# Two network layers in one kernel: one block for both halves, a new opening order, and GpSimd powers in pairs

## The reference, cut to what matters

```python
# first layer
xn = layernorm(x)
s  = silu(xn @ w_gate.T)                    # 1376 wide
s  = keep the larger half of |s| in each row, others 0
s  = (s * (xn @ w_up.T)) @ w_down.T
g  = silu(xn @ ternary(weight).T + bias)
x  = x + s * g
# second layer
xn = layernorm(x)
h  = xn @ Win.T + bin                       # 64 wide
for l in range(4):
    y = silu(layernorm(h, l1w, l1b))
    y = sconv(y)        # y convolved over time with the powers of a complex number p per channel
    h = h + y * sc_lin
    y = layernorm(h, l2w, l2b)
    h = h + silu(y @ W1.T + b1) @ W2.T + b2
s  = layernorm(h) @ Wout.T + bout
g  = silu(xn @ (W + mix of 16 low-rank products).T + bias)
x  = x + s * g
```

## Time and profile before

| | us |
|---|---|
| median of 3 runs | 642.12 (641.61 to 645.01) |
| the profiled execution | 643.55 |
| its span in the profile | 641.7 |
| PE busy | 598.7 (93%) |
| DVE busy | 506.0 (79%) |
| ACT busy | 339.1 (53%) |
| POOL busy | 194.9 (30%) |

### The profile page before, as it was taken

One profiled execution on the slowest core, in us unless ns is written; L12 is line 12 of the kernel. 1 busy time (PEld: TensorE's weight loads), 2 busy tenths in 40 slices (PEclk: granted clock), 3 DMA queues, 4 the chain that ended last, 5 costly groups with the idle time before them and its releaser, 6 DMA issues. The chain is left out here.

```text
span 641.7 us, 8820 instructions
## 1 busy us (share of the span) xinstructions
PE 598.7 (93%) x2852; PEld 464.1 (72%) x2852; DVE 506.0 (79%) x932; ACT 339.1 (53%) x571; POOL 194.9 (30%) x303
## 2 busy tenths in 40 slices
PE   8969999999999999999999999999698899999775
PEld 6857887887888888888888888877566555555432
DVE  7998799897888788789788778677575787877655
ACT  6758477267438428627734752848362444445320
POOL 2422002001001000200200100489884666664334
PEclk9979999999999999999999999999796999999887
DMA  8802000210020030020010001460300000000015
GB/s 359 304 13 67 1 1 1 66 34 2 23 75 0 0 98 0 0 98 0 0 64 34 0 1 67 148 221 4 64 4 0 1 0 1 1 1 1 1 65 196
DMA packets 17194, 32.35 MB, mean 50 GB/s; under 512 B 3238, under 2 KB 3750, under 8 KB 17164
## 3 DMA queue, kind: packets, MB, share of 16 engines
q1 hardware_dynamic: 17164, 31.99, 14.3%
HBM read 24.63 MB, written 7.35 MB: 50 GB/s over the span
## 5 line engine op out<-in xcount | busy, mean ns | idle before, releaser
L857 DVE TENSOR_SCALAR_CACHE_REDUCE junk_d<-k_buf,cand 128x1376 int8<-128x1376 f32 x56 | 91.8, 1640 | 0.3
L650 ACT ACTIVATE junk_a<-k_buf,cand 128x1376 int8<-128x1376 f32 x56 | 80.5, 1437 | 0.6
L1197 PE MATMUL ps_a<-wd_hi,zt_hi 128*128 128x512 f32 (+1 forms) x176 | 71.9, 408 | 0.2 <-DVE zt_lo L976 0.2
L629 ACT ACTIVATE s_buf<-ps_a 128x1376 f32<-128x1376 f32 x16 | 21.1, 1318 | 93.9 <-PE ps_a L1164 89.4
L1197 PE MATMUL ps_a<-wd_hi,zt_lo 128*128 128x512 f32 (+1 forms) x176 | 69.2, 393 | 0.0
L1197 PE MATMUL ps_a<-wd_lo,zt_hi 128*128 128x512 f32 (+1 forms) x176 | 68.8, 391 | 0.0
L527 POOL TENSOR_TENSOR xres<-xres,gate 128x512 f32<-128x512 f32 x12 | 22.4, 1866 | 130.9 <-DVE gate L983 130.9
L519 POOL TENSOR_TENSOR rstd<-var_eps,expo 128x2 f32<-128x2 f32 x7 | 4.9, 706 | 164.9 <-DVE var_eps L779 164.9
L1164 PE MATMUL ps_b<-wu_hi,xt_hi 128*128 128x512 f32 (+1 forms) x192 | 52.4, 381 | 0.0
L1164 PE MATMUL ps_a<-wg_hi,xt_hi 128*128 128x512 f32 (+1 forms) x192 | 52.0, 379 | 0.0
L1164 PE MATMUL ps_a<-wg_lo,xt_hi 128*128 128x512 f32 (+1 forms) x192 | 50.7, 372 | 0.5 <-DVE wg_lo L762 0.4
(11 more groups left out here) (249 smaller groups left out, 1414.7 us busy)
## 6 DMA issues: line engine op xcount, KB each, us to landing
xres<-in_x SPq DMA_DIRECT2D x8, 512.0 KB, 3.3
out<-arena SPq DMA_DIRECT2D x16, 256.0 KB, 2.1
xin<-in_x SPq DMA_DIRECT2D x7, 512.0 KB, 4.0
x_scratch<-xres SPq DMA_DIRECT2D x6, 514.0 KB, 4.0
arena<-x_scratch SPq DMA_DIRECT2D x3, 1028.0 KB, 12.6
m_buf<-in_wg_t SPq DMA_DIRECT2D x2, 688.0 KB, 4.8
k_buf<-in_wg_t SPq DMA_DIRECT2D x2, 688.0 KB, 7.6
m_buf<-in_wu_t SPq DMA_DIRECT2D x2, 688.0 KB, 7.4
```

What stands on the lines that cost most here:

```text
L629: act.activation(s_buf[:, t, :], ps_a[:].rearrange("p a n -> p (a n)")[:, 0:INNER], ACT.Silu).then_inc(s_ready, 1)
L650: act.activation(junk_a[:], k_buf[:, 1, :], ACT.Sign, bias=c, scale=-1.0, accum_out=below[:, 1:2]).then_inc(act_step, 1)
L857: dve.tensor_scalar(junk_d[:], k_buf[:, 0, :], c, -float(DROP), ALU.is_lt, ALU.add, accum_out=e).then_inc(cnt_dve, 1)
L1197: last = pe.matmul(ps_a[:, t, :], zs, ws[0:rows, c, :], start=(c == 0 and n == 0), stop=(c == CHUNKS - 1 and n == 2))
```

## The change

- **One block.** The two blocks become one; each engine runs its first-layer program and then its second-layer program, with no barrier between. The SBUF order of buffers is changed so that `xt`, `row_f`, `row_r`, `ones_r`, `tbig` and the first tables lie over buffers that are free early; `w_down` and what is needed longest lie behind them. `tokens(i)` gets waits for the PSUM banks that the first layer used.
- **TensorE's order.** Token tiles 0 to 2 come ahead of `down(last, 4)`, tiles 3 to 7 ahead of `down(last, 5)`. The opening has two whole gate tiles and eight steps of a third before phase 1 (34 steps for 26). Phase 1 has 31, phases 2 to 6 keep 26, phase 7 has 13.
- **VectorE's order.** `down_gate(last, 0)` follows `take_tile(1)`; `weights_low` and `down_gate(last, 1)` follow `token_stats(0)`. Some splits and the second half of `rows_low` move from the opening to after `h_in(1)`.
- **ScalarE's order.** `weff_hi` comes after the first takes, the Tanh of `rho` after the last down product, and `norm2_apply` of the last four tiles in two twos around the first `norm_out`.
- **GpSimd.** The products of real and imaginary parts go in pairs, 11 instructions for a doubling. All nine doublings run ahead of `residual(last, 0)`; `memset(row_f)` and four table steps come between it and `residual(last, 1)`.
- **SP.** The loads of b1, w1, w2 and wout wait until the last down product is done.

```diff
-N_DOUBLING = 15
+N_DOUBLING = 11
+FIRST_GATES = (2, 9, 7, 9, 2, 2)
+LAST_GATES = (2, 3, 3, 5, 0, 0)
...
-                run(tt(q[0], zr, br, ALU.mult), tt(q[1], zi, bi, ALU.mult),
-                    tt(q[2], zr, bi, ALU.mult), tt(q[3], zi, br, ALU.mult),
-                    tt(t0, e_re, e_re, ALU.mult), tt(t1, e_im, e_im, ALU.mult), tt(t2, e_re, e_im, ALU.mult))
+                zw, by_re, by_im = z[:, :, :, 0:w], tmp[:, 0:2, :, 0:w], tmp[:, 2:4, :, 0:w]
+                run(tt(by_re, zw, br, ALU.mult), tt(by_im, zw, bi, ALU.mult),
+                    tt(e_t[:, 0:2, :], e, e, ALU.mult), tt(t2, e_re, e_im, ALU.mult))
...
-                run(tt(e_re, e_re, t3, ALU.mult), tt(e_im, e_im, t3, ALU.mult))
+                run(tt(e, e, t3.rearrange("p (a l) -> p a l", a=1).to_broadcast([P, 2, DEPTH]), ALU.mult))
...
-                tables_powers(pool, 1, 0, COARSE_BITS - 1)
-                for t in range(2):
-                    residual(PAIRS, t, resident=True)
+                tables_powers(pool, 1, 0, COARSE_BITS)
+                ffn_residual(pool, PAIRS, 0, resident=True)
...
             def recurrent_gpsimd(pool):
...
+                pool.wait_ge(zt_psum, 2 * NG * PAIRS)
                 pool.memset(row_f[:], 0.0).then_inc(rows_zero, 1)
-                tables_powers(pool, 1, COARSE_BITS - 1, COARSE_BITS)
+                pool.wait_ge(q_done, TILES)
+                tables_some(0, 4)
+                ffn_residual(pool, PAIRS, 1, resident=True)
                 norm2_root(pool, 2, LOADED, TILES, expo2[:, 0:TILES - LOADED])
-                tables_some(0, 3)
-                tables_some(3, 6)
                 root(0, 0)
                 pool.wait_ge(ln_w[0], 1)
-                tables_some(6, 8)
+                tables_some(4, 7)
                 times_sin(0, 0, y, ln_o, 1, cv_wi)
                 times_sin(0, 0, u_im, cv_ui, 1, cv_b)
+                tables_some(7, 8)
...
             def recurrent_vector(dve):
...
                 take_tile(1)
+                down_gate(dve, PAIRS, 0)
+                take_tile(3)
+                take_tile(5)
+                take_tile(7)
                 token_stats(0)
-                take_tile(3)
+                for k in range(KH):
+                    weights_low(dve, k)
+                down_gate(dve, PAIRS, 1)
+                dve.wait_ge(bc_ps, 1)
+                dve.tensor_copy(bias_c[:], bank2[0][:, 0:DEPTH + 1]).then_inc(bc_s, 1)
+                dve.wait_ge(bc_s, 1)
+                h_in(0)
                 token_stats(1)
                 token_means()
                 norm2_eps(dve, LOADED, TILES)
-                take_tile(5)
-                take_tile(7)
+                variance(0, 0)
                 norm2_negated(dve, 2, LOADED, TILES)
...
+                split_lo(0)
+                rows_low(32, 0)
+                split_lo(1)
                 weight_means(w2[:], KH, 2 * DEPTH, w2_in, 16, w2_s)
                 widen(0, 0)
                 normed(0, 0)
-                take_means(w2[:], KH, 2 * DEPTH, w2_s)
...
                         h_in(1)
+                        split_lo(2)
+                        take_means(w2[:], KH, 2 * DEPTH, w2_s)
+                        rows_low(32, 1)
+                        rows_low(96, 1)
...
             def recurrent_tensor(pe):
...
-                for i in range(PER_HALF):
+                for i in range(3):
                     tokens(i)
+                down(pe, PAIRS, 4)
+                for i in range(3, PER_HALF):
+                    tokens(i)
+                down(pe, PAIRS, 5)
                 center_biases()
                 project_in(0)
                 for i in range(PER_HALF, PER_HALF + 4):
                     tokens(i)
+                gates(1)
                 variances(0, 0)
-                gates(4)
-                for i in range(PER_HALF + 4, TILES):
-                    tokens(i)
-                gates(9)
+                gates(PRODUCTS)
                 spread(0, 0)
+                gates(7)
+                tokens(PER_HALF + 4)
+                tokens(PER_HALF + 5)
+                gates(3)
+                tokens(PER_HALF + 6)
+                tokens(PER_HALF + 7)
+                gates(3)
                 project_in(1)
-                gates(PRODUCTS + 1)
+                gates(2 * KH)
```

More of the change, by code:

```diff
@@ L546, in _ @@
                     for t in range(2):
-                        residual(p, t)
+                        ffn_residual(pool, p, t)
                 made = [0]
@@ L1130, in last_pair @@
                     zt_low(p + 1, 5)
-                    down_gate(p + 1, 0)
-                    for k in range(KH):
-                        weights_low(k)
-                    down_gate(p + 1, 1)
                 first_pair()
@@ L1140, in _, with down, topk_tensor @@
                 last_pair(PAIRS - 1)
-            @block_a.tensor
-            def _(pe):
+            def down(pe, p, i):
+                t, (c0, c1) = i // NG, GROUPS[i % NG]
+                pe.wait_ge(zt_l, 2 * NG * (p - 1) + i + 1)
+                if isinstance(p, int) and p == 1:
+                    pe.wait_ge(wd_l, len(units) - N_GU)
+                for c in range(c0, c1):
+                    rows = min(P, INNER - c * P)
+                    zh = zt_hi[0:rows, c * P:(c + 1) * P]
+                    zl = zt_lo[0:rows, c * P:(c + 1) * P]
+                    for n, (zs, ws) in enumerate(((zh, wd_hi), (zh, wd_lo), (zl, wd_hi))):
+                        last = pe.matmul(ps_a[:, t, :], zs, ws[0:rows, c, :],
+                                         start=(c == 0 and n == 0), stop=(c == CHUNKS - 1 and n == 2))
+                last.then_inc(down_done, 1)
+            def topk_tensor(pe):
                 def x_transpose(p, t):
@@ L1185, in zt_transpose @@
                     last.then_inc(zt_psum, 1)
-                def down(p, i):
-                    t, (c0, c1) = i // NG, GROUPS[i % NG]
-                    pe.wait_ge(zt_l, 2 * NG * (p - 1) + i + 1)
-                    if isinstance(p, int) and p == 1:
-                        pe.wait_ge(wd_l, len(units) - N_GU)
-                    for c in range(c0, c1):
-                        rows = min(P, INNER - c * P)
-                        zh = zt_hi[0:rows, c * P:(c + 1) * P]
-                        zl = zt_lo[0:rows, c * P:(c + 1) * P]
-                        for n, (zs, ws) in enumerate(((zh, wd_hi), (zh, wd_lo), (zl, wd_hi))):
-                            last = pe.matmul(ps_a[:, t, :], zs, ws[0:rows, c, :],
-                                             start=(c == 0 and n == 0), stop=(c == CHUNKS - 1 and n == 2))
-                    last.then_inc(down_done, 1)
                 def ternary(p, t):
@@ L1340, in _ @@
                 fold_weights(1)
-                down(last, 0)
+                down(pe, last, 0)
                 fold_weights(2)
                 flag(last - 1, 1)
-                down(last, 1)
+                down(pe, last, 1)
                 zt_transpose(last, 2)
@@ L1663, in _ @@
                     q, n = 2 * l, 2 * k + 1
-                    splits = l < DEPTH and 2 * phase + 2 < TILES
                     squares(q, c)
@@ L1681, in _, with recurrent_vector @@
                             hidden(k, d, u)
-                    if splits:
-                        for j in range(2, 4):
-                            split_hi(2 * phase + j)
-            @block_b.vector
-            def _(dve):
+                    for j in range(2 * phase + 3, min(2 * phase + 5, TILES)):
+                        split_hi(j)
+            def recurrent_vector(dve):
                 def take_tile(i):
@@ L1820, in _ @@
                 norm2_eps(dve, LOADED, TILES)
-                take_tile(5)
-                take_tile(7)
+                variance(0, 0)
                 norm2_negated(dve, 2, LOADED, TILES)
-                dve.wait_ge(bc_ps, 1)
-                dve.tensor_copy(bias_c[:], bank2[0][:, 0:DEPTH + 1]).then_inc(bc_s, 1)
-                for k in range(2):
-                    split_lo(k)
-                dve.wait_ge(bc_s, 1)
-                h_in(0)
-                rows_low(32)
-                variance(0, 0)
-                rows_low(96)
+                split_lo(0)
+                rows_low(32, 0)
+                split_lo(1)
                 weight_means(w2[:], KH, 2 * DEPTH, w2_in, 16, w2_s)
```

236 lines of the change are left out of this document (132 added, 104 removed).

## The result

The changed kernel takes 638.28 us (median of 5 runs, 636.95 to 639.29); the kernel before, beside it, 642.12 (5 runs, 641.5 to 645.01). The ratio is 0.9929, with a 95% interval of 0.9901 to 0.9957. It is faster by 3.8 us and not by the 9.1 of the forecast; the time lies within the predicted range, 629.5 to 639.5.

The account below looks back on a forecast made before the run. The chain of waits between engines was taken to bound the kernel, not TensorE's filler. -6.4 - 2.5 - 0.2 = -9.1 us on the profiled 643.55 gave 634.4, less 1.43 for the median 633.0; range 629.5 to 639.5.

Parts of the forecast that it names:

- The opening, -6.4: Seam to phase 1: earlier powers and transposes make h ready at 478.8 against 485.27, 6.4 us sooner.
- 2.48 us for `weights_low`: Opening, VectorE: weights_low takes 2.48 us beside GpSimd's table steps, so product 1 is done by 457.7.
- Phase 1, -2.5: Phase 1 takes 17.4 us against 19.9, with VectorE 1.2 us late to the variance from 2.66 of added work.
- at 6.6 us rather than 5.43: Phase 1: the chain's spread comes 6.6 us into the phase, where later phases have 5.43.
- which also hides the three extra gate steps of fill 1: Phase 1: the later spread covers three added TensorE gate steps, 0.7 us, so they cost nothing.
- Clock high: Phase 1: TensorE keeps its high clock, so the base is 16.2 us as in later phases.
- Phase 7, -0.2: Phase 7: 13 gate steps move out, only the one ahead of the variances is on the chain, 0.2 us saved.
- rival C: Phase 7: with 13 steps fewer TensorE idles 1.4 us and loses its clock, +2 us, 635; chance 0.10.
- The rest: Phases 2 to 6, SBUF order and the added Tanh: 0; w1 and w2 DMAs at most 1 us short.
- B: Opening: the clock falls as TensorE stands 2.3 us ahead of the first spread, +4.6, 637.6; chance 0.20.
- E: Opening: VectorE's waits for GpSimd make it as late as the barrier did, 639.6; chance 0.07.
- project_in needs none of them: Opening: argument that project_in depends on no VectorE wait for GpSimd, only on the takes.

Follow-up runs that it names:

- e11: The changed kernel plus idle products in phases 7 to 9 and 44 idle transposes in the first layer: 632.87 us, ratio 0.985.
- e4: The kernel before with the paired powers alone (11 instructions a doubling), still two blocks: 639.9 us, ratio 0.9964.
- e5: The changed kernel with the powers unpaired again (15 instructions a doubling): 640.88 us, ratio 0.9984.
- e7: The changed kernel with only the filler behind phase 1's variances thinned, FIRST_GATES (2, 5, 9, 11, 2, 2): 639.15 us, ratio 0.9942.
- e3: The changed kernel with take_means and two rows_low moved from ahead of phase 1's first variance to later places: 638.03 us, ratio 0.9916.
- e6: e3 plus thinner filler behind phase 1's variances, FIRST_GATES (2, 5, 9, 11, 2, 2): 635.38 us, ratio 0.9897.
- e8: e6 with GpSimd's table steps shifted one place later so none lies beside into_h: 635.35 us, ratio 0.9914.
- e10: e8 plus idle products in phases 7 to 9 and 44 idle transposes near 32 us in the first layer: 630.98 us, ratio 0.9831.
- a0: The changed kernel run again, unaltered, beside the first follow-up runs: 636.55 us, ratio 0.991.

## Why the prediction was right in sign and wrong in size

*The opening, -6.4: right.* It measured -6.35, and seven profiles with this opening lie within 0.03 us of each other (32.44 to 32.47); the eighth, e11, has 32.60. This execution's first layer ended 0.9 later; with that taken off, the powers end at 450.9 (forecast 450.6), project_in(0) starts at 455.6 (455.6), the turn at 470.0 (470.3). TensorE stands 0.30 us ahead of `center_rows`. e4 and e5 show that both parts of the change are in it.

One step inside it was mis-sized, and its cover hid that. I took 2.48 us for `weights_low`, from a stretch in which GpSimd did powers of 4 and 16 elements; here it lies beside 512-element table steps and takes 5.30. So product 1 ends at 461.3, less the 0.9 460.4, and not at 457.7, and residual 1 ends 1.0 later than forecast. The splits, rows and means ahead of `widen` gave that back: 464.83 to 467.67, 2.8 us where I had 3.3 to 3.8, and small steps the rest. The Trainium skill (SBUF — State Buffer, SBUF: two separate sides) says that a VectorE instruction with two SBUF inputs and a GpSimd instruction that reads SBUF exclude each other for their whole length. The trace agrees roughly: one of the four took 0.68 us and the longest 1.77. By that rule the term would have been, as an estimate, 2.48 and nearly three table steps of 1.07, some 5.7.

*Phase 1, -2.5: the step that failed; it was -1.2.* The forecast put VectorE 1.2 us late to its variance; it was 2.3 late (4.98 after `center_rows` against 2.65). The means and the two `rows_low` take 3.23 us (481.64 to 484.87), where my 2.66 had 1.98 for them beside the split: this one price was 1.25 short, and it was taken from rows without GpSimd's table step (1.53 at 481.33) beside them. The forecast's spread "at 6.6 us rather than 5.43" came at 7.90. e5 and e7 show that this lateness alone makes it so. Behind it stood a second error that cost nothing here: "which also hides the three extra gate steps of fill 1" holds at 2.4 GHz, but at 1.2 GHz they reach to 7.65 by themselves (e3). So either cause alone accounts for the phase's 18.6 to 18.7, taking one away shows nothing, and taking both gives 17.20 (e6), or 17.73 to 18.47 where the clock falls (e8 to e10). "Clock high" was wrong as well: of the eleven profiles with the new opening and paired powers, ten show a fall in phase 1 (all but e6). In the first profile it cost nothing: counted from h, 18.74 with the fall and 18.74 without one in e5. In e11 it came earlier, lasted longer, and the phase took 19.84.

*Phase 7, -0.2: right while the clock is up (15.18, -0.23, in a0), +1.3 in the profiled execution.* This is rival C, to which I gave 2 us and a chance of 0.10. It cost 1.5. A fall in full in two of seven profiles and a short one in two more suggest that the chance was too low. The same kernel shows the fall in one execution and not in another: it should have been a term of the sum with a share, not a rival.

*The rest.* Phases 2 to 6 gave 0.0 as forecast. DMAs of w1 and w2 cost nothing that a row shows. The Trainium skill (ScalarE: Activation LUTs, What ACT_TABLE_LOAD costs) gives 2.66 us to every change to another table set. The trace has no such time at this Tanh, which takes 0.19 us and leaves no gap; whether a change of set is due there no run here shows, so the page's figure was not put to the test. B (a fall in the opening) did not happen in any profile of the change with paired powers; e5 shows it when TensorE stands 3.09. E did not happen in them either, but its "project_in needs none of them" left out `tokens(10)`, which waits for `down_gate(last, 1)`: 0.18 us in the changed kernel, 3.09 in e5.

*The sum.* In the spans the change gave 5.0 for 9.1. The 4.1 missing are 1.3 in phase 1, the price that was short; 1.5 in phase 7, the fall that the sum put at nothing; and 1.25 at the start and behind phase 7, which it also put at nothing. The medians show 3.8, for two more reasons. The sum took the profile of before to lie 1.43 above its median; that of the changed kernel lies 0.53 above its own. And it took the time around the span as unchanged: 1.73 to 1.87 us in every run of before, e4 and e5, it is 2.04 to 2.15 in every run of a kernel that has both the one block and the paired powers. Where these 0.3 us come from is open.

6.35 + 1.21 + 0.23 = 7.8 us is what the change saves, against this profile of before, where the clock stays up in phase 7. That execution took 643.55 at a mean granted clock of 0.966; four others of the kernel, at 0.979, took 639.38 to 641.13. No trace of one of these was kept, so a part of the 7.8 may belong to that one execution. a0's profiled span is 9.3 us under the profiled span of before, the forecast's size, but 1.4 of it lies behind phase 7, in code that the change leaves alone: a single execution would have confirmed the forecast by luck. By the medians a0 is 6.6 under before (643.13 to 636.55), the first comparison 3.8. What lies between these and 7.8 is probably when the clock falls in phase 7 and at the end; e10, which holds it up at the start and the end, lies 4.4 us under e8. Which share each place has in the medians stays open.

## What to carry to other kernels

Price a moved VectorE operation beside what GpSimd will be doing at its new place, not by the row at its old one, and price filler at half clock as well, ahead of whatever is queued behind it. Where two queues reach a point late by about the same, test the two edits together: one at a time each looks worthless. And when a kernel's runs scatter by 4 us, look at the stretches of low clock: idle products in the few long TensorE gaps gained 4.4 us here (e8 to e10), about as much as the whole reordering (3.8 and 6.6).

## What the runs showed of the hardware

- A VectorE operation on two 512-element SBUF operands takes 0.62 us on the mean beside GpSimd's powers of 4 and 16 elements and 1.33 beside its 512-element table steps (2.48 and 5.30 for four); `take_means` takes 0.68 in e3, where GpSimd has its root beside it, and 1.77 in the changed kernel beside a table step.
- TensorE's granted clock fell to 1.2 GHz at about 484.2 in phase 1 of the changed kernel (0.72 over 484.0 to 484.5), 2.4 us after TensorE had gone back to work, with 0.77 us of standing ahead of that and 0.30 before. In e6 the same order of work up to that point kept 1.00. The same 1.12 us of idle in phase 7 came with a fall in one execution and with none in another. The Trainium skill (TensorE: Matmul & The Clock Gate, Part 1: The HAM clock gate) says that the point of the change varies between runs; the traces agree. Two executions of one kernel lie 4.3 us apart here, 1.5 of them by the fall in phase 7.
- 44 idle transposes over 4.96 us of TensorE's standing at 32 us keep the clock at 1.00 over 34 to 45 in e10, where e8 has 0.69. In e11 the same transposes leave 0.84.
